# Macaron block on one core: expert places by tiles, the attention's first step reordered, setup memsets in front, down casts out of the second routing

## The reference, cut to what matters

```python
x = hidden                                     # (8, 1024, 256)
x = x + 0.5 * ffn(layernorm(x))
x = x + attention(layernorm(x))
x = x + 0.5 * ffn(layernorm(x))

def ffn(tokens):                               # 8192 tokens, E = 8 experts, CAP = 320
    probs = softmax(tokens @ gate_w)
    expert = argmax(probs)
    mask1 = one_hot(expert, E)
    pos = cumsum(mask1, axis=0) - 1            # place of a token within its expert
    sec_mask = mask1[:, :, None] * one_hot(pos, CAP)
    expert_input = einsum('tec,td->ecd', sec_mask, tokens)
    h = relu(einsum('ecd,edf->ecf', expert_input, w1))
    return einsum('tec,ecd->td', probs[:, :, None] * sec_mask, einsum('ecf,efd->ecd', h, w2))

def attention(x):                              # per chunk of 128 steps, batch 8, D = 64
    g = gradient of |silu(k W1^T) W2^T - v|^2, clipped to norm 1
    per step t:  S = eta_t * S - theta_t * g_t;   W = (1 - alpha_t) * W + S
    h = silu(q_t W1_t);  out_t = h W2_t        # with the W of each step
```

## Time and profile before

| | |
|---|---|
| median of 3 runs | 769.07 us (767.38 to 770.98) |
| profiled execution | 769.89 us |
| its span, first to last instruction | 768.1 us |
| mean granted TensorE clock | 0.956 |
| busy, share of the span: PE, DVE, ACT, POOL | 87%, 79%, 57%, 31% |
| stages | first routing 0 to 55, experts 55 to 198, attention 198 to 601, second routing 601 to 618, experts 618 to 768 us |

### The profile page before, as it was taken

One profiled execution on the slowest core, in us unless ns is written; L12 is line 12 of the kernel. 1 busy time (PEld: TensorE's weight loads), 2 busy tenths in 40 slices (PEclk: granted clock), 3 DMA queues, 4 the chain that ended last, 5 costly groups with the idle time before them and its releaser, 6 DMA issues. The chain is left out here.

```text
span 768.1 us, 15489 instructions
## 1 busy us (share of the span) xinstructions
PE 670.9 (87%) x5715; PEld 579.7 (75%) x5715; DVE 608.2 (79%) x1373; ACT 437.8 (57%) x1105; POOL 238.6 (31%) x201
## 2 busy tenths in 40 slices
PE   4619999999597889999999999999998369999996
PEld 2218889898476777988879888887976257989985
DVE  0777888873389999999999999999985959887851
ACT  1415585571357647677666877767463546557550
POOL 0033543113211417053350714416061053722202
PEclk9858999999799999999999999999999769999999
DMA  9959727250311003113040221302103815834401
GB/s 334 395 202 358 239 87 254 77 173 29 117 56 55 1 1 120 47 55 111 9 158 1 89 78 56 110 2 66 47 1 110 273 47 167 281 96 166 130 15 35
DMA packets 58226, 89.26 MB, mean 116 GB/s; under 512 B 6960, under 2 KB 49072, under 8 KB 58032
## 3 DMA queue, kind: packets, MB, share of 16 engines
q1 hardware_dynamic: 46176, 70.28, 26.8%
q0 software_dynamic: 3840, 10.49, 4.1%
q10 hardware_dynamic: 8144, 7.61, 3.3%
HBM read 74.73 MB, written 22.02 MB: 126 GB/s over the span
## 5 line engine op out<-in xcount | busy, mean ns | idle before, releaser
L715 PE MATMUL ps<-moe_normedT_high,weights_high_up 128*128 128x320 f32 x252 | 80.4, 319 | 0.8 <-DVE moe_hidden_low L536 0.7
L716 PE MATMUL ps<-moe_normedT_low,weights_high_up 128*128 128x320 f32 x252 | 77.8, 309 | 0.0
L717 PE MATMUL ps<-moe_normedT_high,weights_low_up 128*128 128x320 f32 x252 | 77.8, 309 | 0.0
L1227 POOL TENSOR_TENSOR att_o_rs<-att_o_mean,minus_half 128x4 f32<-128x4 f32 x16 | 16.2, 1012 | 195.9 <-DVE att_o_mean L1486 195.9
L715 PE MATMUL ps<-weights_high_down,moe_hidden_high 128*128 128x256 f32 x256 | 73.4, 287 | 0.0
L536 DVE SCALAR_TENSOR_TENSOR moe_hidden_low<-ps,moe_hidden_high 128x256 fp32r<-128x256 f32 x128 | 53.8, 420 | 23.9 <-ACT moe_hidden_high L673 19.6
L717 PE MATMUL ps<-weights_high_down,moe_hidden_low 128*128 128x256 f32 x256 | 71.5, 279 | 0.0
L716 PE MATMUL ps<-weights_low_down,moe_hidden_high 128*128 128x256 f32 x256 | 71.4, 279 | 0.0
L632 ACT CAST weights_high_down<-weights_raw_down 128x256 fp32r<-128x256 f32 x96 | 35.1, 407 | 39.8 <-PE ps L717 26.5
L715 PEld LDWEIGHTS ps<-weights_high_down,moe_hidden_high 128*128 128x128 f32 x256 | 48.0, 188 | 3.1 <-issue 3.1
L312 DVE TENSOR_TENSOR weights_low_down<-weights_raw_down,weights_high_down 128x256 fp32r<-128x256 f32 x128 | 49.7, 414 | 0.0
(11 more groups left out here) (328 smaller groups left out, 2072.0 us busy)
## 6 DMA issues: line engine op xcount, KB each, us to landing
weights_raw_up<-in_w SPq DMA_DIRECT2D x16, 1024.0 KB, 8.9
weights_raw_down<-in_w SPq DMA_DIRECT2D x16, 1024.0 KB, 8.5
first_xt<-in_xT SPq DMA_DIRECT2D x8, 1024.0 KB, 7.8
weights_rows<-x SPq DMA_DIRECT2D x8, 1024.0 KB, 5.5
out_x<-weights_rows SPq DMA_DIRECT2D x8, 1024.0 KB, 4.6
weights_rows<-x ACTq DMA_DIRECT2D x7, 1024.0 KB, 5.5
weights_rows<-x SPq DMA_DIRECT2D x2, 512.0 KB, 4.2
weights_raw_up<-in_w_x SPq DMA_DIRECT2D x1, 768.0 KB
```

The costliest lines, as they stand in the source:

```text
L715: mm(dst, high_l, high_r, start=start, stop=False)
L716: mm(dst, high_l, low_r, start=False, stop=False)
L717: return mm(dst, low_l, high_r, start=False, stop=stop)
L1227: g.tensor_tensor(o_rs[:, n], o_mean[:, n], t["minus_half"][:, n], ALU.pow).then_inc(o_rs_ready, 1)
```

## The change

`place` is stored as tiles by experts, as the onehot is. The add of L142 now writes with a stride; L147 and L149 work on elements in a row. In the second routing ScalarE does 11 up casts, `partitions`, the 5 other up casts; the 16 down casts stand at the head of ScalarE's queue in the second layer's expert block. `first_high` takes single pieces and waits before each. `start()` runs before the first statistics. In the first step of the attention the gradients come ahead of the two scans, and P2 ahead of the first gates and the momentum scan; the other steps keep their order.

```diff
@@ Router.__init__
-        self.place = sb("place", [P, E, n])
+        self.place = sb("place", [P, n, E])
@@ Router.slots
-        v.tensor_tensor(place[:], cum.rearrange("p (e n) -> p e n", e=E), self.running[:, :, 0:n],
+        v.tensor_tensor(place[:].rearrange("p n e -> p e n"), cum.rearrange("p (e n) -> p e n", e=E),
+                        self.running[:, :, 0:n],
                         ALU.add).then_inc(chain, 1)
...
-        v.tensor_tensor(place[:], place[:], onehot.rearrange("p n e -> p e n"), ALU.mult).then_inc(chain, 1)
+        v.tensor_tensor(place[:], place[:], onehot, ALU.mult).then_inc(chain, 1)
         dve.wait_ge(chain, c + 9)
-        v.tensor_reduce(pos[:], place[:].rearrange("p e n -> p n e"), AX.X, ALU.add).then_inc(chain, 1)
+        v.tensor_reduce(pos[:], place[:], AX.X, ALU.add).then_inc(chain, 1)
@@ route, scalar
-            weights.first_high(act, weights.UNITS[0:2])
+            weights.first_high(act, UP_PIECES[:11])
             router.partitions(act)
-            weights.first_high(act, weights.UNITS[2:4])
+            weights.first_high(act, UP_PIECES[11:])
@@
+UP_PIECES, DOWN_PIECES = ([(u, f) for u in ((unit, 0), (unit, 1)) for f in range(KF)] for unit in ("up", "down"))
@@ Weights
-    def first_high(self, act, units=UNITS):
-        for u in units:
+    def first_high(self, act, pieces):
+        for u, f in pieces:
             act.wait_ge(self.loaded[u], 16)
-            for f in range(KF):
-                self.nc.scalar.copy(...)
+            self.nc.scalar.copy(...)
@@ experts, scalar
+            if not gathers_made:
+
+                weights.first_high(act, DOWN_PIECES)
             for i in range(2):
                 first_high_tiles(i)
@@ first_route, scalar
-            weights.first_high(act)
+            weights.first_high(act, UP_PIECES + DOWN_PIECES)
@@ memory_attention, first_stats
                 moments_of(0, range(HALF, B))
-                start()
@@ memory_attention, step
                 thetas(c, par)
+                gradients(c, par)
                 if first:
                     carry_scans(c, True)
                     decay_scans(c, True)
-                gradients(c, par)
...
+                if first:
+                    second_scores(c, par)
                 gates(c + 1, 1 - par, (0,), first)
                 momentum_scans(c + 1)
-                second_scores(c, par)
+                if not first:
+                    second_scores(c, par)
@@ memory_attention, vector
+            start()
             first_stats()
```

More of the change, by code:

```diff
@@ L301, in gather @@
                                               bounds_check=TOK - 1, oob_is_err=False).then_inc(self.gathered[i], 16)
-    def first_high(self, act, units=UNITS):
-        for u in units:
+    def first_high(self, act, pieces):
+        for u, f in pieces:
             act.wait_ge(self.loaded[u], 16)
-            for f in range(KF):
-                self.nc.scalar.copy(self.piece(self.high, u, f), self.piece(self.raw, u, f)
-                                    ).then_inc(self.high_done[u], 1)
+            self.nc.scalar.copy(self.piece(self.high, u, f), self.piece(self.raw, u, f)
+                                ).then_inc(self.high_done[u], 1)
     def low_piece(self, dve, g, u, f):
```

## The result

The kernel with all four edits takes 766.46 us (median of 20 runs) against 769.11 of the kernel before (20 runs beside them): −2.65 us, ratio 0.9968 with a 95% interval of 0.9953 to 0.9983, so −3.6 to −1.3 us. Forecast were −6.3 us. Two further series gave 0.9988 (0.9966 to 1.0011) and 0.9984 (0.9945 to 1.0024). The intervals of these two hold no change at all. Over the three series the change gains some 1 to 3 us, less than half of what was forecast.

The account below looks back on a forecast made before the run. The prediction saw TensorE bounding the experts, VectorE the attention steps, and chains of small instructions the stretches between. −0.7 − 1.8 − 2.4 − 1.4 = −6.3 us from the 769.07 median gave 762.8 us, range 761.2 to 766.8.

Parts of the forecast that it names:

- several rivals: Range's upper end: partial loss (764.9 us, chance 0.13) joined to strided writes (0.22) and TensorE's clock falling (0.12).
- P2 ahead: Attention's first step: P2 before the gates waits 0.45 us and lets TensorE's retrieval start at once; with gradients, −1.4 us.
- the rule by which the gains were added up: All four edits sit in or beside chains that set the time, so their gains add in full: −6.3 us.
- the taps' collision: First step: first query taps on VectorE meet GpSimd's mixing products; 1.35 us of the gradients' 2.2 us saving taken back.
- the fourth gate's wait: First step: VectorE's 1.04 us wait for the fourth gate pair falls away, as P2 ahead brings that pair forward.
- Places: Place table by tiles: product and sum cheaper, add unchanged; −0.37 us a block in the first routing, 0.72 in the second's chain.
- Strided writes pay: Rival, chance 0.22: the new add costs 0.19 us more per first-routing block and 0.37 in the second; total 763.5 us.
- Second routing: Shorter VectorE chain, earlier partition product, and down casts moved behind the block bring the release forward: −1.8 us.
- Memsets in front: Attention entry: setup memsets before the first statistics let GpSimd's first power start earlier: −2.4 us, bounds −1.6 and −2.4.

Follow-up runs that it names:

- places_only: Kernel before with only the place table laid out by tiles; untimed, one profile: 16.69 us from marks to release in the second routing.
- after: Kernel with all four edits, first profile and series, against the kernel before: 766.46 us against 769.11, ratio 0.9968.
- after_again: The same kernel with all four edits, profiled and timed a second time against the kernel before: ratio 0.9988 (0.9966 to 1.0011).
- after_third: The same kernel with all four edits, profiled and timed a third time against the kernel before: ratio 0.9984 (0.9945 to 1.0024).
- no_p2_ahead: Kernel with all edits except P2 ahead: second scores stay behind gates and momentum scan; ratio to the kernel before 0.9939 (0.9919 to 0.9959).
- gates_then_p2: All edits, but in the first step the first gate pair precedes P2, which stays ahead of the momentum scan; ratio to the kernel before 0.9944.
- padded_more: no_p2_ahead plus an unread 128x448 VectorE copy behind the second routing's sum; untimed, 16.09 us from marks to release.

## Why the prediction was wrong

The direction was right, but the size, −6.3 us, is not what was measured (−2.65). The median lies in the range, near its upper end, where several rivals had to come together; that is not a hit of the mechanism. Two steps failed in mechanism, P2 ahead and the rule by which the gains were added up; two terms were mis-sized.

- **P2 ahead**, forecast to join the gradients for −1.4 us: "What it buys is TensorE's time". It costs time, 1.2 us in the step where the clock stays up, 3.4 where it falls, and by the medians of one series 2.9 us of the total (767.43 against 764.55 without it). Its wait was put at 0.45 us; it was 1.02 and 2.70. VectorE came to P2 1.1 us sooner than it came to the gates before (forecast 0.85; the taps' collision cost 0.47 where 1.35 was taken back, and some 0.6 went in pieces of 0.1 elsewhere), but the products ended 1.20 us later (forecast 0.9). And I booked 1.04 us for the fourth gate's wait as if P2 ahead alone could remove it: with the gradients ahead and P2 behind, five of six profiles have no such wait. The gradients alone bring the step from 74.2 us (mean of seven) to 71.9, or to 72.87 where the clock falls: 1.3 to 2.3 us. Against the two of the seven in which nothing waited, 73.17 and 73.20, they bring 1.3, and gradients and P2 together 0.1.
- **"A microsecond taken from such a chain moves all that comes later, because every later wait is for an event that moves too."** Later waits are for TensorE, and TensorE's pace changes with its granted clock (0.42 and 0.70 us for the same four products in the first step). Second experts: 0.17 to 0.35 us more from the turn to the first low hidden tile in all ten profiles with the place edit and ten products, and some 0.57 us to the middle where nothing else waited; places_only has it with this edit alone, so it goes with the edit, by a path that stays open. Last step: +1.1 in two of three profiles (not shown to come from the edits). The first routing's block 0: its gain ended in a wait for logits in the first profile.
- **Places**: mis-sized as the rival *Strided writes pay* had it, by 0.20 a block and 0.39 us; −0.17 a block instead of −0.37 in the first routing (and block 0's only where no wait for logits follows), and 0.30 instead of 0.72 in the chain of the second. That the one strided write in the trace, a memset of eight elements, showed no toll said nothing of a large one.
- **Second routing**: −1.8 forecast, −1.28 in the pair; most of the difference is the strided write (0.39). But a typical execution of the kernel before has no late partition product: there it is −0.65. One execution's late landing went into the forecast as if it were the rule.
- **Memsets in front**: −2.4 forecast, −2.53 in the pair. Right in mechanism and place. That the size fits is in part luck: the power came 2.19 us sooner, and the rest is TensorE's turns at a higher clock, which no term of the sum held.

With typical values: −0.2 to −0.3 (first routing), −2.5 (entry), −0.65 (second routing) and +0.57 (second experts) make about −2.8 us. The first step adds −1.1 (73.09 against 74.2) in the executions of after and after_again and +2.0 (75.32 and 0.9 in the next) in that of after_third, the last step +1.1, +1.1 and 0: −2.8, −2.8 and −0.8 us. The three series measured −2.65, −0.9 and −1.2 (the last two by their ratios). The same count for no_p2_ahead gives −2.8 − 2.3 = −5.1 us, measured −4.7 (−6.2 to −3.2), and for gates_then_p2 −4.6, measured −4.3. The count is of one execution each and the series are of many, so that it comes near is support, not proof; for after_again it is off by 1.9 us.

## What to carry to other kernels

When an edit takes time from a chain that ends in TensorE's work, don't book it before the work behind it is shown to keep its pace; and read the price of a wait from several executions, since one with a fallen clock or a late transfer makes a wait look like a rule. Of two edits that aim at the same wait, try each alone: here one gave 1.3 to 2.3 us by itself and the other took 1.2 us of it back. An instruction that is put ahead of the work that hides its input's arrival turns every delay of that input into idle time of the engine that sets the step.

## What was not expected of the hardware

- A write of 4-byte elements 32 bytes apart costs VectorE as much as a strided read: 0.62 against 0.42 us (256 elements), 1.08 against 0.69 (512).
- Behind gaps of the same length TensorE's granted clock fell in some executions and stayed in others: in the first step, with 1.92 to 1.96 us, in 2 of 10 profiles; in the last step, with 1.93 us, in 4 of 20; ahead of the first step's retrieval, with 2.72 to 2.77 us, in 5 of 7. In the second experts' entry it fell in all ten profiles with the place edit and ten products, in none of the other ten.
- VectorE's copy of 448 elements of 4 bytes, put behind the sum, took 0.38 us in the trace and moved the next instruction by 0.18 us (0.90 us behind the sum's start in padded_more, 0.72 in no_p2_ahead); the gather index moved by 0.02, since VectorE's wait for TensorE ahead of it shrank from 0.67 to 0.51.
